# Decoder stack with 40 attention batches: the loads of stacked keys before those of queries, the first queries of the second attention earlier, and two statistics behind the first maxima

## The reference, cut to what matters

```python
x = x + L0_xattn(layernorm(x), ctx)          # A0: 16 heads of 8, softmax(q k^T / sqrt(8)) v
x = x + L0_ffn(layernorm(x))                 # F0: 8-bit weights, 16-bit activations, gelu, 128 -> 512 -> 128
x = x + L1_xattn(layernorm(x), ctx)          # A1
x = x + L1_ffn(layernorm(x))                 # F1: 8 experts, best 2, and a shared one, gelu
x = x + L2_xattn(layernorm(x), ctx, mask)    # A2: with a mask of 256 x 512
x = x + L2_block(layernorm(x))               # AS: causal self-attention; F2: 8 gated experts, best 2, silu
x = x + L3_xattn(ctx, layernorm(x), mask)    # A3
x = x + L3_ffn(layernorm(x))                 # F3: 8 experts, best 2, gelu, and a layernorm
```

## Time and profile before

| | |
|---|---|
| timed runs, median of 3 | 1792.91 us (1792.71 to 1793.48) |
| profiled execution | 1801.7 us, its span 1799.9 us |
| TensorE busy | 1690.6 us, 94% of the span |
| VectorE, ACT, GpSimd busy | 62%, 60%, 35% |
| mean granted TensorE clock | 0.969 of full speed |
| scores of A0 begin | at 20.58 us |
| scores of A1 begin | at 301.21 us |
| loads of keys, of queries | 128 of 256 KB and 32 of 128 KB; 160 of 128 KB |

### The profile page before, as it was taken

The page is one execution under the profiler, slowest core; times in us unless marked ns, Lnnn a source line. Parts: engine busy times, 40 slices in busy tenths (PEclk is TensorE's granted clock), DMA queues, the critical chain, the costliest instruction groups (busy, mean ns, idle before and its releaser), DMA issues.

```text
span 1799.9 us, 38537 instructions
## 1 busy us (share of the span) xinstructions
PE 1690.6 (94%) x14287; PEld 1133.4 (63%) x14322; DVE 1119.9 (62%) x3293; ACT 1071.3 (60%) x2147; POOL 637.2 (35%) x1050
## 2 busy tenths in 40 slices
PE   7999978999999999999999999989998999999998
PEld 3555545455568988854444455568885555489997
DVE  5788958888832232357777676646667888633332
ACT  2788852888864444447777755443335888744443
POOL 4454333344332223223444443223353454222221
PEclk9999988899999999979999999989998999999999
DMA  5344203455200000213332244300032654000000
GB/s 169 122 136 147 76 24 96 131 176 154 74 7 1 1 1 19 77 59 95 108 89 87 60 137 123 90 1 1 1 105 65 184 162 121 13 1 7 7 7 7
DMA packets 114852, 132.35 MB, mean 74 GB/s; under 512 B 14934, under 2 KB 78700, under 8 KB 114668
## 3 DMA queue, kind: packets, MB, share of 16 engines
q1 hardware_dynamic: 114668, 129.90, 23.8%
HBM read 83.45 MB, written 46.40 MB: 72 GB/s over the span
## 4 chain that ended last, share of the span: by engine, by line
PE 79%; ACT 9%; DVE 5%; issue 4%; POOL 2%; DMA 1%; SPq 0%; POOLq 0%; DVEq 0%; ACTq 0%
PE ps_s L1424 16%; PE ps_av L1280 14%; PE ps_s L1237 11%; PE ps_t L1400 10%; ACT prob L986 6%; PE ps_t L1253 4%; PE ps_s L1400 4%; PE ps_t L1264 3%; PE ps_m L1327 2%; PE ps_m L1336 2%; PE ps_m L1321 2%; PE ps_m L1314 1%; PE ps_m L1289 1%; PE ps_m L1349 1%; PE ps_t L1266 1%
## 5 line engine op out<-in xcount | busy, mean ns | idle before, releaser
L986 ACT ACTIVATE prob<-ps_t 128x512 f32<-128x512 f32 (+1 forms) x1152 | 616.1, 588 | 188.4 <-PE ps_t L1253 182.2
L1716 DVE TENSOR_REDUCE mx<-ps_s 128x1 f32<-128x512 f32 x752 | 474.2, 683 | 83.0 <-PE ps_s L1237 81.3
L1237 PE MATMUL ps_s<-kst,qst 32*128 32x512 f32 (+2 forms) x1248 | 382.4, 486 | 16.9 <-DVE mx L1716 8.7
L1253 PE MATMUL ps_t<-qmx,kst 32*128 32x256 f32 (+1 forms) x2304 | 333.9, 341 | 23.2 <-ACT prob L986 20.3
L1424 PEld LDWEIGHTS ps_s<-w_ffn,prob 128*128 128x128 f32 x2688 | 317.8, 194 | 10.6 <-issue 3.4
L1424 PE MATMUL ps_s<-w_ffn,prob 128*128 128x128 f32 x2688 | 324.4, 278 | 0.0
L1280 PE MATMUL ps_av<-prob,vaug 128*32 128x256 f32 (+1 forms) x4608 | 311.0, 389 | 3.2 <-ACT avs L1027 3.2
L1237 PEld LDWEIGHTS ps_s<-kst,qst 32*128 32x128 f32 x1248 | 166.4, 190 | 176.8 <-issue 96.6
L1173 ACT ACTIVATE prob<-ps_t,b1c 128x512 f32<-128x512 f32 x204 | 125.5, 686 | 238.6 <-PE ps_t L1400 238.6
L2006 DVE SCALAR_TENSOR_TENSOR acc<-ps_s,comb,acc 128x128 f32<-128x128 f32 x336 | 94.6, 345 | 259.1 <-PE ps_s L1424 259.1
L1253 PEld LDWEIGHTS ps_t<-qmx,kst 32*128 32x128 f32 x2304 | 201.9, 190 | 61.1 <-ACT prob L986 52.2
(11 more groups left out here) (240 smaller groups left out, 2258.6 us busy)
## 6 DMA issues: line engine op xcount, KB each, us to landing
kst<-k_parts SPq DMA_DIRECT2D x128, 256.0 KB, 3.5
qst<-q_parts SPq DMA_DIRECT2D x160, 128.0 KB, 3.6
k_parts<-k_hi SPq DMA_DIRECT2D x64, 256.0 KB, 3.0
q_parts<-q_hi SPq DMA_DIRECT2D x80, 128.0 KB, 2.4
ctxT<-in_ctxT SPq DMA_DIRECT2D x32, 256.0 KB, 2.7
k_parts<-k_lo SPq DMA_DIRECT2D x32, 256.0 KB, 3.1
q_parts<-q_lo SPq DMA_DIRECT2D x40, 128.0 KB, 2.4
w_ffn<-in_F_w SPq DMA_DIRECT2D x18, 256.0 KB, 2.9
```

What stands on the lines that cost most here:

```text
L986: nc.scalar.activation(row[:, S * kt:S * kt + w], ps_t[TURN[unit(ph, g, n) % 8]][:, 0:w], ACT.Exp).then_inc(sig["exp_done"], 1)
L1237: pe.matmul(dst, qst[p][strip, g, q * 128:(q + 1) * 128], kst[p][strip, g, 0:nk], start=True, stop=True).then_inc(sig["s_ready"], 1)
L1253: mm = pe.matmul(dst, kst[p][strip, g, kt * 128:(kt + 1) * 128], qmx[strip, g % 2, seen(ph, kt):], start=not opened, stop=not opened or c ...
L1716: dve.tensor_reduce(mx[:, buf, i:i + 1], src, AX.X, ALU.max, negate=True).then_inc(sig["max_done"], 1)
```

## The change

Four edits, none of which changes what is computed.

1. `load_strips` issues the four key loads first, before it waits for the saved queries, and then the four query loads. Before, it waited for both saves and issued the loads in pairs. This holds for all 40 batches.
2. In F0, TensorE does Q of A1's batch 0 right behind XT of that batch. Before, one output block stood between them.
3. VectorE takes the statistics of the last block (two halves) behind the 16 first maxima of A1. Before, they stood in front of them.
4. GpSimd makes the two `rstd` of that block behind the split of group 1's maxima. Before, they stood in front of group 0's.

```diff
@@ load_strips (SP)
                 sp.wait_ge(k_saved[p], saved(ph, bt))
+                for g in range(NG):
+                    sp.dma_start(kst[p][:, g, 0:nk].bitcast(F32), scratch["k"][p][128 * g:128 * (g + 1), 0:nk]).then_inc(stacked[p][g], 16)
                 sp.wait_ge(q_saved[p], saved(ph, bt))
                 for g in range(NG):
-                    sp.dma_start(kst[p][:, g, 0:nk].bitcast(F32), scratch["k"][p][128 * g:128 * (g + 1), 0:nk]).then_inc(stacked[p][g], 16)
                     sp.dma_start(qst[p][:, g, :].bitcast(F32), scratch["q"][p][128 * g:128 * (g + 1), :]).then_inc(stacked[p][g], 16)
@@ attention (GpSimd), head of A1
                     split_maxima(ph, b0, 1)
+                    if ph == "A1":
+                        for half in range(2):
+                            power("F0", NBLK - 1, half, (NBLK - 1) * TB + half * QT, QT)
@@ F0 (GpSimd)
-                    for blk in range(1, NBLK):
+                    for blk in range(1, NBLK - 1):
                         for half in range(2):
                             power(ph, blk, half, blk * TB + half * QT, QT)
@@ quantised_ffn (TensorE)
                 for n in range(2 * NBLK):
                     output(n // 2, n % 2)
-                    what = {3: ("XT", 0), 4: ("Q", 0)}.get(n)
-                    if what:
-                        misc(what[0], "A1", Batch(what[1]))
+                    if n == 3:
+                        misc("XT", "A1", Batch(0))
+                        misc("Q", "A1", Batch(0))
@@ attention (VectorE)
                         for i in range(8):
                             maximum(ph, b0, g, i)
+                if ph == "A1":
+                    new_statistics(NBLK - 1, 0)
+                    new_statistics(NBLK - 1, 1)
@@ quantised_ffn (VectorE)
                 add(3, 1)
-                new_statistics(3, 0)
-                new_statistics(3, 1)
```

More of the change, by code:

```diff
@@ L1860, in rounded, with new_statistics @@
                 return dve.tensor_scalar(dst, dst, ROUND, A16, ALU.subtract, ALU.min)
+            def new_statistics(blk, half):
+                wait(dve, "x_new", cnt.at("x_new", "F0", blk, half))
+                n = 2 * blk + half
+                all_statistics([x_tok[:, QT * n + q, :] for q in range(QT)], QT * n)
             def quantised_ffn():
@@ L1901, in add @@
                                              in1=dst, op0=ALU.mult, op1=ALU.add).then_inc(sig["x_new"], 1)
[L1903 to L1906, removed]
                 def first_tokens():
```

## The result

The changed kernel took 1816.21 us (median of 4, 1802.12 to 1824.32) beside 1792.81 of the kernel before: a recorded ratio of 1.0102, interval 1.0063 to 1.0142. Timed again in the first experiment it took 1810.89 (9 executions), ratio 1.0084, 1.0050 to 1.0117. The forecast was 1794.1, in a range of 1791.4 to 1796.4, with 7% for "slower".

The account below looks back on a forecast made before the run. TensorE, busy 94% of the span, was taken as the bound, with load waits only at the starts of A0 and A1. A0 +1.25 and A1 -0.9 + 0.83 gave +1.15 us: 1794.1, range 1791.4 to 1796.4.

Parts of the forecast that it names:

- the steady batches: In 38 of 40 batches loads are asked for a batch ahead, so their order costs nothing.
- A0: Start of A0: query 0 lands behind 1,024 KB of keys instead of 256, 1.25 us later.
- A1's start: Start of A1: query saves 2.0 us earlier, mostly lost to keys first; first maximum 0.9 us earlier.
- The statistics: A1, between the maxima of groups 1 and 2 on VectorE: 0.83 us later for everything behind.
- up to 0.4 comes back; I count none: A1: possible gain if GpSimd's two moved powers were what held VectorE between groups; not counted.
- AS: Phase AS goes on from A2 with no wait on a load; no cost counted.
- Rival 2: A1: a shorter standstill at 298 to 300 us keeps the clock at 2.4 GHz, 3 us gained, 1791.1; 8%.
- a wait on a load shows up in a batch that had none: One of the signs listed as proving the forecast wrong, for the profile after; no size given.
- Rivals 1 and 4: 1: first queries don't queue behind keys, 1792.3 us, 15%. 4: A1's query product comes no earlier, 1796.3 us, 4%.
- Rival 3: A0 and A1: loads run at 200 GB/s or less and the save is held up, +4.0 us, 1796.9; 8%.
- The yardstick: A measurement of this kernel can tell about 0.2%, 3.6 us, from no change.
- parts 2 and 3: A1: part 2 is edit 2, the earlier query product; part 3 is edits 3 and 4, the moved statistics, 0.83 us later.

Follow-up runs that it names:

- r1: The changed kernel itself timed once more, no edit, against the kernel before: 1810.89 us, ratio 1.0084.
- r2: The changed kernel without edit 1 (loads in key and query pairs in all phases), against the kernel before: 1796.91 us, ratio 0.9983.
- r7: The kernel before with edit 2, and in AS query loads asked for ahead of the keys' save; statistics in their old place: 1794.17 us, ratio 0.9991.
- r3: The changed kernel with load pairs in AS alone, keys first elsewhere, against the kernel before: 1801.66 us, ratio 1.0033.
- r12: The kernel before with edit 2 alone, pairs everywhere and statistics in their old place: 1794.36 us, ratio 0.9985.
- r8: The kernel before with edit 1 alone, keys ahead of queries in all five attention phases: 1812.20 us, ratio 1.0070.
- r4: The kernel before with keys first in AS alone: 1810.37 us, ratio 1.0064.
- r5: The kernel before, in AS alone four key loads, then queries 3, 2, 1, 0, so the first group's queries come last: 1837.25 us, ratio 1.0221.
- r6: The kernel before, in AS alone four query loads ahead of the wait for the keys' save, then four keys: 1796.98 us, ratio 1.0007.
- A0 alone: The kernel before with keys ahead of queries in phase A0 alone: 1803.46 us, ratio 1.0032.

## Why the prediction was wrong

**The step that failed** is the one on the steady batches: "38 of the 40 batches the loads are hidden, since they are asked for a batch ahead, and their order among themselves costs nothing there", and "AS goes on from A2, and no wait on a load stands there". The rows said truly that no wait stood there. They didn't say how near one was: 1.1 to 2.1 us. The change moves the first query load back behind the first key load, by 1.4 us in most batches of AS and 2.2 in AS2. I read the absence of a wait as cover without measuring the cover, and took four phases as one: in AS the order of the saves is turned round (written in the code: `save_k` behind `save_q`), which takes the change's only gain and leaves its price. Had I set that shift, 1.4 us from the issues and more where they come slowly, against the slack of the tightest phase, the sum would have had up to seven more places.

**The sum, term by term.** A0: +1.25 forecast, +1.1 in the trace after and up to 2.2 in others; right in its mechanism (the first query load does stand behind 1,024 KB of keys). From key 0 landed to query 0 landed, 896 KB by the prediction's count, it took 2.85 us in the trace after and 3.5 to 4.0 in the four others, forecast 3.4. A1's start: its pieces pulled as said, in smaller size. The query product came 0.6 us earlier against the last add in after, r1, r2 and r7, 1.7 in r3 and r12, and not 2.0, and keys first took more than that back, so that scores begin 2.8 us after the last add's start (r3: 2.0) in place of 1.7; I had them 0.8 after it. The term has the wrong sign. The statistics cost the 0.83 of the forecast; but 0.37 came back in front of the ninth maximum, net +0.47. The prediction had named such a gain from the moved powers ("up to 0.4 comes back; I count none"); all five traces with part 3 have it, though no run moves the powers alone. AS: 0 forecast; on the mean of the traces 125.4 - 118.9 = 6.5 us in six batches, some 2.5 of it waits and the rest time at half clock, nearly all of that from one trace (r8, 17 us over the kernel before). Together 1.1 to 2.2, 1.1, 0.5 and 6.5 make 9 to 10 us, at the low end of the 9 to 21 that the interval of r1 allows; with the 3.0 of the three other traces it is 6 to 7, and misses it. That AS loses 6 to 17 us is timed (r4's interval), not added up from traces.

**The rivals.** Rival 2 named the clock, but as a gain, at A1 alone. None had a wait in AS; "a wait on a load shows up in a batch that had none" stood only among the things that would prove me wrong. It did. Rivals 1 and 4 fall with the traces of A0 and of the query product; the clock after 301 stayed at half, as before, so rival 2 fell too. Rival 3 had the right sign and the wrong place: at A0 no trace shows its 4.6 us for the 896 KB. Of the working, two readings are slightly off: rows 5 had two query loads of A1 at 5.8 us, not one, and rival 3's A0 term is 2.8 by its own numbers, not 2.6. Neither moves the forecast.

**The yardstick** was wrong too: I took three close executions for the scatter of the kernel. With intervals of ±0.25% from 12 executions, parts 2 and 3 can't be told from nothing, and none of r2, r7 and r12 is shown to beat the kernel before, though all three lie 0.1 to 0.2% below it.

**What stays open.** That the order of the loads in AS makes the kernel slower is shown (r4 against before), and that the order with the later first query costs more (r5). That the standstill brings the half clock is argued, from r6, where keys in a row without the wait do no harm, and from the long stretches behind 2.52 us in r5 and 0.60 in r8. Against it stand waits of the same length without a fall, and the two stretches of 34 us in r5 with no load wait ahead of them. Why a stretch of half clock lasts 3 us in one execution and 44 in another isn't known, nor why A0 alone measured 0.32% for 2.2 us in its trace.

## What to carry to other kernels

- That nothing waits for a load doesn't make it free to be later. Read when it landed and when its reader began, in the phase where the batches are shortest, and set the shift against that difference.
- A load order that pays where keys are saved first has nothing to give where they are saved last: check the order of the saves in each phase before one loop over loads is changed for all.
- A standstill of TensorE of half a microsecond may cost more than itself: behind 0.60 us one batch took 10 us longer, while others of that length cost only themselves. Compare stretches of the same work and their granted clock, over several executions, before a total is believed.

## What the runs showed of the hardware

Half clock held on while TensorE worked without a break: 29.38 of 29.70 us busy at a granted clock of 0.51 (AS5 in r8), in a stretch that lasted 44 us. The Trainium skill (TensorE: Matmul & The Clock Gate, "Part 1: The HAM clock gate") says that the gate follows how busy the engine was: idle it falls to 1.2 GHz, kept at work it comes back to 2.4. The first half agrees with r5 and r8, where half clock sets in within a wait of 2.52 us and behind one of 0.60, but not with r5's later stretches, ahead of which TensorE was never idle longer than 0.31. The second doesn't hold in these stretches.

One kernel's executions differed by up to 23 us (1789.56 to 1812.38 for the kernel before), and the traces show the same instructions with half clock in other places. From 65 us on, where every trace has records of the clock, it is 89 us in all in r12, 113 before, 110 in the changed kernel's profiled execution (its shortest), 147 in r8, 226 in r5.

A granted clock of 1.00 at the start of a trace can be a missing record: in the kernel before, r9 and r12 the first stands at 62 to 64 us, and the products with the values take 634 ns each between 40 and 58 us and 385 between 70 and 80. The mean of 0.969 for the kernel before leaves that out.
